# Memory of lines in a macaron layer: a blend and a clip moved in VectorE's order, tails and first copies moved, the decayed state computed by ScalarE

## What is computed

```python
write_lines = exterior(w1, w2)                      # 6 numbers a head, divided by their norm
read_lines = exterior(r1, r2)
Jw = jnp.einsum('bthi,ij->bhtj', write_lines, _J6)
outer = Jw[..., :, None] * Jw[..., None, :]         # 6 x 6 a head and position
M_cumsum = jnp.cumsum(outer * decay_inv[...], axis=2)   # shifted by one position
M_all = M_cumsum * decay_fwd[...]
rd_M = jnp.einsum('bhti,bhtij->bhtj', rd, M_all)
score_M = jnp.sum(rd_M * rd, axis=-1)
score_M2 = jnp.sum(rd_M * rd_M, axis=-1)
mem_score = (1 - alpha) * score_M + alpha * score_M2
```

## Time and profile before

| what | value |
|---|---|
| median of 3 executions | 1931.45 us (1929.91 to 1931.5) |
| profiled execution, its own time | 1929.68 us |
| its span | 1927.9 us |
| busy share of the span | PE 96%, DVE 83%, ACT 77%, POOL 48% |
| bodies 0 to 5 of the stage, on DVE | 1151.06 to 1229.34 us |

### The profile page before, as it was taken

The page is one execution under the profiler, slowest core; times in us unless marked ns, Lnnn a source line. Parts: engine busy times, 40 slices in busy tenths (PEclk is TensorE's granted clock), DMA queues, the critical chain, the costliest instruction groups (busy, mean ns, idle before and its releaser), DMA issues. The chain is left out here.

```text
span 1927.9 us, 61303 instructions
## 1 busy us (share of the span) xinstructions
PE 1859.5 (96%) x22646; PEld 1110.0 (58%) x22646; DVE 1603.4 (83%) x5457; ACT 1490.9 (77%) x4110; POOL 920.6 (48%) x552
## 2 busy tenths in 40 slices
PE   7999999999999999999999998889999999999999
PEld 3777773577775343444433357536777635777754
DVE  5999975899995669999999949969999658999945
ACT  4999994699997362777777764359999947999973
POOL 2888860488882050000000035448888505888820
PEclk9999999999999996999999999999999999999999
DMA  5212130121221041111111000002222201121311
GB/s 178 51 44 50 44 69 6 29 50 44 50 63 29 1 155 34 42 42 41 42 41 42 25 7 2 2 19 45 49 47 48 62 6 35 44 50 44 69 23 44
DMA packets 76266, 85.29 MB, mean 44 GB/s; under 512 B 17151, under 2 KB 50755, under 8 KB 75843
## 3 DMA queue, kind: packets, MB, share of 16 engines
q1 hardware_dynamic: 75775, 81.37, 17.0%
q10 hardware_dynamic: 196, 0.02, 0.0%
HBM read 20.83 MB, written 8.39 MB: 15 GB/s over the span
## 5 line engine op out<-in xcount | busy, mean ns | idle before, releaser
L336 ACT ACTIVATE probs<-probs,negmax 128x128 f32<-128x128 f32 x1024 | 401.7, 401 | 1.5 <-DVE negmax L411 1.2
L2330 ACT ACTIVATE gprobs<-ps_global 128x1024 f32<-128x1024 f32 (+3 forms) x384 | 291.4, 811 | 125.4 <-PE ps_global L1764 102.8
L291 POOL TENSOR_TENSOR rot<-rot 128x1024 f32<-128x1024 f32 x128 | 302.4, 2362 | 144.3 <-DVE rot L381 144.3
L297 POOL TENSOR_TENSOR qk<-rot,cnorm 128x1024 f32<-128x1024 f32 x128 | 243.8, 1905 | 172.2 <-issue 149.5
L304 POOL TENSOR_TENSOR probs<-probs,iden 128x1024 f32<-128x1024 f32 x128 | 242.8, 1897 | 46.5 <-DVE iden L419 45.9
L2009 DVE TENSOR_REDUCE maxes<-ps_global 128x1 f32<-128x512 f32 (+2 forms) x384 | 222.0, 637 | 10.9 <-PE ps_global L1727 6.5
L411 DVE CUSTOM_DVE_ANT_0 probs<-ps_attn,masks 128x128 f32<-128x128 f32 x1024 | 226.0, 284 | 0.6 <-issue 0.5
L1722 PE MATMUL ps_global<-kq 48*128 48x512 bf16 (+3 forms) x768 | 197.6, 347 | 6.8 <-DVE maxes L2009 1.6
L336 ACT ACTIVATION_READ_ACCUMULATOR probs<-probs,negmax 128x1 f32 x1024 | 203.9, 199 | 0.0
L2247 POOL CAST m_parts<-m_turn 32x128 bf16<-32x128 f32 x16 | 4.5, 280 | 364.3 <-DVE m_turn L2023 364.3
L377 DVE TENSOR_TENSOR rot<-ps_attn,rotary 128x512 f32<-128x512 f32 x256 | 174.8, 683 | 2.7 <-PE ps_attn L202 2.3
(11 more groups left out here) (233 smaller groups left out, 4494.4 us busy)
## 6 DMA issues: line engine op xcount, KB each, us to landing
v_first<-v_second SPq DMA_DIRECT2D x256, 128.0 KB, 2.3
hs<-z_a SPq DMA_DIRECT2D x256, 32.0 KB, 1.9
ln<-z_b SPq DMA_DIRECT2D x56, 128.0 KB, 2.3
kq<-split_scratch SPq DMA_DIRECT2D x64, 96.0 KB
kq<-split_scratch SPq DMA_DIRECT2D x64, 64.0 KB
split_scratch<-parts SPq DMA_DIRECT2D x8, 384.0 KB, 4.4
split_scratch<-gprobs SPq DMA_DIRECT2D x6, 384.0 KB, 3.9
x_tok<-in_x_dram SPq DMA_DIRECT2D x4, 512.0 KB, 5.9
```

The source lines that it names most:

```text
L291: nc.gpsimd.tensor_tensor(a, a, b, ALU.add).then_inc(C["rot_sum"], 1)
L297: nc.gpsimd.tensor_tensor(qk[:, k % 2, :].rearrange("p (h d) -> p h d", d=DH), rot_a[:, k % 2, :, :], cnorm[:, k % 2, :].unsqueeze(2).to_b ...
L336: last = nc.scalar.activation(probs[:, k % 2, slot, :], probs[:, k % 2, slot, :], ACT.Exp, scale=-1.0, bias=negmax[:, k % 2, slot:slot + 1 ...
L2330: nc.scalar.activation(probs[:, step % RING, 2 * p:2 * p + 2, 0:w], ps[:, S0 + 2 * p:S0 + 2 * p + 2, 0:w], ACT.Exp).then_inc(C["p2_exp"], 1)
```

## The change

- DVE: the clip of the reading line (`clip(t+2, 1)`) moves from the end of body t to the place behind the first `terms` of body t+1. The sum of squares 1 goes to the very end of the body, behind `advance`. The sum of squares 0 moves behind the second `read_memory`, and the multiplies of items 6 and 7 move ahead of it.
- DVE and ACT: `advance(k)` for k > 0 no longer multiplies the state by `whole`. ACT does that into a new buffer `faded` (`fade`, four activations of 144 elements), and DVE adds the tails in two additions of 288 elements. `advance` waits for `fade`, which waits for the `advance` before.
- PE: `tails(t+1)` moves behind line items 6 and 7.
- ACT: the copies of items 0 and 1 of the next tile move from the start of a body to the place ahead of the second inverse norm of the body before; all of items 5 to 7 are copied ahead of the first square; `fade` stands behind the copy of the scores.

```diff
@@ tensor, body
                 memories(5, 6)
+                lines(6, 8)
                 if t + 1 < LAST:
                     tails(t + 1)
-                lines(6, 8)
@@ vector, advance
+                if k > 0:
+                    wait(dve, "ml_faded", k)
+                    for half in range(2):
+                        at = slice(half * GROUPS // 2, (half + 1) * GROUPS // 2)
+                        last = nc.vector.tensor_tensor(state[:, (k + 1) % 2, at, :].rearrange("p q n -> p (q n)"),
+                                                       faded[:, at, :].rearrange("p q n -> p (q n)"),
+                                                       ps[:, TAIL_BANKS[half], 0:2 * STATE_ROWS], ALU.add)
+                    last.then_inc(C["ml_state"], 1)
+                    return
@@ vector, body
                 multiplies(0, 1)
                 all_terms(0, 1)
+                if 1 < t + 1 < S_TILES:
+                    clip(t + 1, 1)
                 multiplies(1, 2)
...
                 all_terms(5, 6)
+                multiplies(6, 8)
+                if valid(t):
+                    read_memory(t, 1)
                 if valid(t + 2):
                     sum_squares(t + 2, 0)
-                if valid(t):
-                    read_memory(t, 1)
-                multiplies(6, 8)
                 if valid(t):
                     weigh(t)
                 if valid(t + 2):
                     clip(t + 2, 0)
-                    sum_squares(t + 2, 1)
                 if t + 1 < LAST:
                     advance(t + 1)
                 if valid(t + 2):
-                    clip(t + 2, 1)
+                    sum_squares(t + 2, 1)
@@ scalar
+            def fade(k):
+                wait(act, "ml_state", k)
+                for q in range(GROUPS):
+                    last = nc.scalar.activation(faded[:, q, :], state[:, k % 2, q, :], ACT.Identity, scale=A["whole"][:, q:q + 1])
+                last.then_inc(C["ml_faded"], 1)
@@ scalar, body
-                lefts(0, 2)
+                if t == 0:
+                    lefts(t, 0, 2)
                 if valid(t - 2):
                     copy_scores(t - 2)
-                lefts(2, 5)
+                if 0 < t + 1 < LAST:
+                    fade(t + 1)
+                lefts(t, 2, 5)
                 if valid(t):
                     scale_lines(t)
-                lefts(5, 6)
+                lefts(t, 5, 8)
                 if valid(t + 2):
                     square_line(t + 2, 0)
-                lefts(6, 8)
-                if valid(t + 2):
                     inverse(t + 2, 0)
                     square_line(t + 2, 1)
+                lefts(t + 1, 0, 2)
+                if valid(t + 2):
                     inverse(t + 2, 1)
```

More of the change, by code:

```diff
@@ L1560, in global_attention_pass @@
             "ml_outer", "ml_tail", "ml_state", "ml_row0", "ml_row1", "ml_m", "ml_term", "ml_read", "ml_plain", "ml_blend", "ml_weight",
-            "ml_score", "ml_turned", "ml_out"))
+            "ml_score", "ml_turned", "ml_out", "ml_faded"))
     U2 = P2_STEPS
@@ L1584, in global_attention_pass @@
         later = sb("later", [P, CHUNK])
+        faded = sb("faded", [P, GROUPS, B * LINE * LINE])
         ps = ctx.enter_context(nc.psum_tensor(C.own("ps_global"), [P, 8, CHUNK], F32))
@@ L2415, in body, with lefts @@
             def body(t):
-                def lefts(first, end):
+                def lefts(t, first, end):
                     if valid(t + 2):
```

## The result

The changed kernel takes 1934.55 us in the median (11 executions, 1931.21 to 1937.34). The kernel before, executed beside it again, now has a median of 1928.98 (11 executions, 1926.78 to 1931.50), 2.5 us under the median of the three shown first. The ratio is 1.0027 [1.0019, 1.0035]: **0.27% slower, 5.2 us** (5.6 between the two medians), where the forecast was no change. The profiled execution has a span of 1933.8 us and its own time is 1935.58.

What follows compares the result with a forecast made beforehand. DVE was taken as the bound (busy 12.15 of 12.83 us a body); its 1.59 us savings turn into waits in a 12.93 us loop, in all 0.0 (-0.3 to +0.5) on the median 1931.45: 1931.5 us, range 1928.3 to 1934.5.

Steps and rivals of the forecast that it cites:

- Slower by over 0.2%: Whole kernel: the outcome of a time more than 0.2% above the kernel before, given 13%; same had 81%.
- What DVE saves: DVE, each body: shorter state step 0.36, no wait for ACT's square 0.55, no `weigh` collision 0.68; together 1.59 us.
- The loop: From tails to tails through row transfers, memory, line items and DVE: 12.93 us a tile, against 12.83 now.
- rival 1: DVE stays the bound, all gained: 1923.5, 6%; rows landed at once leave about 12.3 a loop, 1928.3, 6% more.
- PE's clock: PE standing still 2 us a body might halve its rate in memory and line items: 15 us, 1946, 8%.
- Rival 3: PE's clock falls behind each row wait; loop grows some 3 us, five loops make 15: 1946, 8%.
- The landing of the rows: Row transfers behind the tails: SP starts 0.12 after their end, issues for 2.40, rows land 1.09 later.
- Rival 2: Rows land later in each loop: 0.35 x 5 = 1.8 us, 0.3 at the last memory, 1933.6; 17%.
- Behind body 5: Tile 7's late clip: last rows land at 1241.7, PE arrives at 1241.89; covered by 0.15 us, nothing or up to 0.3.
- `fade`: ACT, early in the body: four activations of 0.32, 1.3 us (0.8 to 2.5), costing nothing while the row wait covers it.

Runs made afterwards that it cites:

- e1: The changed kernel with one row transfer a tile instead of four: 1925.13 us, 0.9977 of the kernel before.
- e3: The kernel before with only the tails moved behind line items 6 and 7: 1930.23 us, ratio 1.0004.
- e6: The changed kernel without `fade`, the state's step as before in four fused DVE instructions: 1935.19 us, ratio 1.0034.
- e9: The changed kernel run once more, unaltered, for a second trace: 1932.98 us, ratio 1.0024.
- e10: The changed kernel with the clip of tile 7 back at the end of body 5, ahead of the reciprocal: 1932.62 us, ratio 1.0017.
- e12: The kernel before with the tails behind items 6 and 7 and only the last tile's clip moved behind the reciprocal and first terms: 1935.56 us, ratio 1.0035.
- e2: The kernel before with one row transfer a tile instead of four: 1929.70 us, ratio 1.0001.
- e4: The changed kernel with seven matmuls of overwritten result ahead of the row wait in tiles 1 to 6: 1930.83 us, ratio 1.0009.
- e7: The kernel before with only `fade` on ACT and the two additions on DVE: 1925.70 us, ratio 0.9986.
- e8: The changed kernel with the tails back at their early place, ahead of items 6 and 7: 1937.55 us, ratio 1.0043.
- e11: The changed kernel with one row transfer a tile and the last clip ahead of the reciprocal: 1925.58 us, ratio 0.9983.

## Where the prediction was right and where it was wrong

The median is 1934.55, 3 us above the forecast and at the upper edge of the range, 1934.5. That it comes so near is luck: the forecast was built on 1931.45, and against its own neighbour (1928.98) the change costs 5.6 us where 0.0 was forecast. "Slower by over 0.2%" had 13%. By the forecast's own steps:

- **What DVE saves: right.** 0.56 for `weigh`, 0.81 for the additions, no wait ahead of the first sum. DVE's busy time is 11.37 in body 3 and 11.54 in body 4, not 11.24: five and seven of its instructions stand behind a wait there, without the 0.08 by which neighbours overlap. The wrong number cost nothing, DVE isn't the bound.
- **The loop: right.** 12.93 forecast, 13.02 measured, with PE idle 1.90 ahead of the memory and the row transfer as what ends it. e1 shows that this is the tie: 1.64 off the landing brings the loop to 12.12, near the 12.3 that rival 1 gave as the limit of early rows. e3 shows that the moved tails alone make it.
- **PE's clock: the step that failed.** Rival 3 was priced as all or nothing, five loops of 3 us, and given 8% because one idle time of 2.22 us had not brought the clock down. The runs show a case between: of the 30 waits of 1.87 to 2.92 us in six profiles with late tails and four transfers (the changed kernel, e3, e6, e9, e10, e12), 11 were followed by a half-rate memory, of between 3.78 and 4.14 us, and 19 by one of 2.47. Where PE waits 1.17 or less ahead of these memories (the kernel before, e1, e2, e4, e7, e8 and e11, 35 of them) none is at half rate; behind the 3.76 to 3.79 ahead of tile 6's memory all six are. One row that goes the good way says little of a thing that happens in a third of the cases. In the changed kernel's profile this is 3.34 of the 5.26 us, and e4, which fills the wait, takes 3.68 off the reciprocal. The Trainium skill, "TensorE: Matmul & The Clock Gate", section "HAM oscillation — how this bites in real kernels", describes a loop whose transfer wait, longer than the ones here, sends the array back to half rate in each turn. In this case it was one to three turns of five.
- **The landing of the rows: mis-sized.** A constant 3.61 behind the tails' end was taken; it is 4.41 and 4.33 in two loops, 1.5 us in all. Rival 2 had nearly the sum (1.8), but spread over all loops, and it looked for the cause in a longer issue. In these two the issue takes 2.46 and 2.41, and the rows come 1.84 and 1.80 behind its end instead of 1.09.
- **Behind body 5: half right.** The rows came 12.74 behind the reciprocal (forecast 12.4), 0.3 of it a late landing again (3.92 behind the outer products' end, where e6 and e12 have 3.59 and 3.58), and against the kernel before this costs 0.2. But the cover was no fixed work: part of it was the gates at half rate, behind PE's 3.92 us of idle time (2.88 for 1.90). In the new order PE would be there 1.94 sooner, and it waits. So the late clip takes away what the new order would have given back: 1.85 us from e3 to e12 (10.57, 12.42), 2.6 from e10 to e9 (10.11, 12.75), of which e10 pays 0.79 elsewhere.
- **`fade`: right.** 1.33 us for four (forecast 1.3), and covered, by 0.40 of ACT's idle time in a body at full rate; e6 gains nothing without it. The prediction's estimate of 1.25 takes off four overlaps where four instructions have three; with its figures it is 1.32. Moreover e7 gains 3.1 us by this part alone, 2.6 of which the trace shows. In the new order its 0.36 a body turns into waits; in the old one, where DVE is the bound, part of it is real.

**What each part is worth**, then: `fade` alone -3.1 us; the change without the tails' move is the worst form (e8, +8.8); the tails moved alone are +4.1 up to the reciprocal and -2.0 behind it in the trace, +0.8 timed and not told from nothing (e3); the whole change is +5.6. With one row transfer in place of four the same change is the best kernel here, e1: 1925.13, 9 us under the changed kernel and 4.3 under the one before. e7 is as fast within the intervals.

**What stays open:** which of the waits the clock falls behind. Lengths of 1.87 to 1.92 are on both sides, and in the same program tile 1 was at half rate behind 2.92 and at full rate behind 2.70 (e9). And the last clip's price isn't borne out by times: e10's 1.5 us isn't resolved in its timed runs, and e12 lies further above e3 than its trace explains.

## What to carry to other kernels

Before moving an instruction of the bound engine, follow what hangs behind it through the transfer queues once round the loop: here two lines of PE's order turned DVE's 1.6 us of savings into a wait, and the cure was not another order but a shorter transfer path (one issue of 0.50 for four that take 2.40 together). A new wait on PE is priced twice, as the time and as a chance of half rate for the work behind it; price the chance by how often it may happen, not as all or nothing. And when a term is "covered" by 0.15 us, look at what the cover is: if it is a stall or slow running of the old order, it goes when the order changes.

## What the runs showed of the hardware

**Rows that land late have a packet of the instruction queue beside them.** With four transfers the rows that PE waits for land 3.61 to 3.67 us behind the tails' end or 3.97 to 4.41, nothing between. The DMA queues of the changed kernel in the stretch of its first late row, 1160.5 to 1165.0 (packets, MB, share):

```profile
q1 hardware_dynamic: 32, 0.01, 0.8%
q14 instruction: 1, 0.01, 0.8%
```

and in the next loop, 1175.9 to 1180.0, where the row is in time:

```profile
q1 hardware_dynamic: 32, 0.01, 0.9%
```

One packet of the queue "q14 instruction" falls into the first and none into the second. I went through all of them in the kernel before, the changed one, e3, e4, e6, e8, e9, e10 and e12: the 17 late rows each have such a packet in the stretch, and none of those in time has one (packets of "q8 instruction" make no difference). With `fade` and late tails together it hits tiles 1 and 5 each time (4.41 and 4.33, in e4 4.22 and 4.18, in e9 4.20 and 4.16, in e10 4.31 and 4.33); in e3, e6 and e12, without `fade`, neither. Tile 6 has it in all of them. The packet isn't there just because a late stretch is longer: it starts 1.8 to 3.0 us behind the tails' end, inside the 3.61 of a row in time. In the changed kernel it comes at 1.85 in tile 6, during the issue, which takes 2.75 with the usual 1.09 behind it; in tiles 1 and 5 it comes at 3.01 and 2.96, behind the issue, and there the landing is longer. That a fetch holds the transfer up is argued from this, not tried by itself.

**The issue is most of four small transfers in a row.** Four copies of 2.2 KB each take 2.40 us to issue one after the other and are there 1.09 later; one copy of all four partitions takes 0.50 and is there 1.97 behind the tails' end, in all.
